# A Perceiver layer: the queries of tiles 5 to 15 projected in three rounded passes

## The reference

```python
x = x + xattn(layernorm(x), ctx_1024, lens, Wq, Wk, Wv, Wo, q_norm_w, k_norm_w)
x = x + attn(layernorm(x), w_qkv, w_out)      # sparse causal mask, 16 heads
x = x + ffn(layernorm(x), w_gate, w_up, w_down)   # 4-bit weights, 16-bit activations

def xattn(q, kv, lens, Wq, Wk, Wv, Wo, q_norm_w, k_norm_w):   # q (32,64,128), kv (32,1601,128)
    qh, kh, vh = heads(q @ Wq), heads(kv @ Wk), heads(kv @ Wv)   # 16 heads of 64
    qh, kh = rms_norm(qh, q_norm_w), rms_norm(kh, k_norm_w)
    scores = einsum('bhld,bhsd->bhls', qh, kh) / 8
    scores = where(arange(1601) < lens, scores, -1e9)
    return merge(softmax(scores) @ vh) @ Wo
```

## Time and profile before

| what | value |
|---|---|
| median of 3 executions | 2392.42 us (2389.41 to 2395.27) |
| the profiled execution, its own time | 2390.12 us |
| its span in the profile | 2388.3 us |
| array busy | 2322.5 us, 97% of the span, 16519 matmuls |
| VectorE, ScalarE, GpSimd busy | 2096.7, 1363.6, 1485.5 us |
| query stage: first to last carry in the array's timeline | 30.16 to 119.83 us |
| mean granted clock of the array | 0.997 |

### The profile page before, as it was taken

How to read it: one execution, slowest core, us unless ns; L and a number is a source line. 1 busy time by engine, 2 the same in 40 slices (tenths; PEclk the granted TensorE clock), 3 DMA queues, 4 the chain that set the end, 5 groups by cost and what they waited for, 6 DMA issues and landing times. The chain is left out here.

```text
span 2388.3 us, 57754 instructions
## 1 busy us (share of the span) xinstructions
PE 2322.5 (97%) x16519; PEld 1967.9 (82%) x16519; DVE 2096.7 (88%) x3382; ACT 1363.6 (57%) x2594; POOL 1485.5 (62%) x1069
## 2 busy tenths in 40 slices
PE   7989999999999999999999999999999998999988
PEld 4757888888888888888888888888888888878755
DVE  8799999999999999999999999999999998468777
ACT  5845555555555555555555555555555554355646
POOL 4556777777777777777777777777777773001100
PEclk9999999999999999999999999999999999999999
DMA  3522222222222222222222222222222214431000
GB/s 112 194 78 47 55 54 54 54 55 54 56 53 54 54 57 54 54 52 56 55 55 54 54 54 54 54 54 54 54 54 54 54 39 123 149 107 38 2 2 18
DMA packets 442654, 145.07 MB, mean 61 GB/s; under 512 B 365361, under 2 KB 425681, under 8 KB 442449
## 3 DMA queue, kind: packets, MB, share of 16 engines
q1 hardware_dynamic: 442432, 143.50, 24.2%
q10 hardware_dynamic: 144, 0.52, 0.1%
HBM read 109.17 MB, written 34.73 MB: 60 GB/s over the span
## 5 line engine op out<-in xcount | busy, mean ns | idle before, releaser
L472 POOL TENSOR_TENSOR probs<-arena,best_all 128x1024 f32 (+2 forms) x397 | 943.4, 2376 | 422.6 <-DVE best L849 402.8
L1114 PEld LDWEIGHTS u_ps<-rows,probs 128*128 128x128 f32 x6656 | 800.5, 192 | 55.8 <-issue 14.7
L1114 PE MATMUL u_ps<-rows,probs 128*128 (+1 forms) x6656 | 811.4, 275 | 10.1 <-ACT probs L677 5.0
L834 DVE SCALAR_TENSOR_TENSOR arena<-s_ps,mask,rrms 128x512 f32 (+2 forms) x832 | 603.4, 726 | 116.4 <-PE s_ps L978 115.0
L677 ACT ACTIVATE probs<-probs 128x1024 f32<-128x1024 f32 (+1 forms) x416 | 440.8, 1061 | 411.5 <-POOL probs L472 397.8
L809 DVE TENSOR_REDUCE ssq<-squares 128x16 f32<-128x1024 f32 (+2 forms) x416 | 490.2, 1178 | 34.2 <-ACT squares L635 33.2
L635 ACT ACTIVATE squares<-k_ps 128x512 f32<-128x512 f32 (+1 forms) x832 | 451.2, 591 | 40.9 <-PE k_ps L978 21.4
L849 DVE TENSOR_TENSOR best<-best,arena 128x1024 f32<-128x1024 f32 (+1 forms) x352 | 446.7, 1269 | 0.4 <-issue 0.2
L976 PE MATMUL k_ps<-w_hi,cT_hi 128*128 128x512 f32 (+1 forms) x832 | 362.4, 436 | 4.8 <-ACT squares L635 4.8
L629 ACT ACTIVATE cT_hi<-cT 128x128 fp32r<-128x128 f32 (+1 forms) x416 | 129.3, 311 | 370.3 <-DVE cT L800 370.2
L976 PE MATMUL s_ps<-q_hi,cT_hi 128*128 (+2 forms) x832 | 330.5, 397 | 3.2 <-DVE arena L834 3.0
(11 more groups left out here) (257 smaller groups left out, 2236.7 us busy)
## 6 DMA issues: line engine op xcount, KB each, us to landing
stage<-in_ctx SPq DMA_DIRECT2D x1536, 16.0 KB, 1.7
rows<-in_ctx SPq DMA_DIRECT2D x32, 768.0 KB
queries<-probs SPq DMA_DIRECT2D x16, 1024.0 KB, 4.1
q_plain<-queries SPq DMA_DIRECT2D x32, 512.0 KB, 3.3
best_all<-best_rows SPq DMA_DIRECT2D x31, 512.0 KB, 3.6
u_transposed<-uT_sb SPq DMA_DIRECT2D x124, 128.0 KB, 2.6
a_uT<-u_transposed SPq DMA_DIRECT2D x10, 1024.0 KB, 4.9
arena<-u_transposed SPq DMA_DIRECT2D x6, 1024.0 KB, 4.9
```

What stands on the lines that cost most here:

```text
L472: pool.tensor_tensor(probs[0:r, slot_of(c, PRING), :], scores_at(b, c), best_all[0:r, bass.ds((b % 2) * HL, HL)], ALU.subtract).then_inc(s ...
L834: dve.scalar_tensor_tensor(out=scores_at(p, c, h * HALF, HALF).rearrange("p (h l) -> p h l", l=L), in0=s_ps[h][0:r, :].rearrange("p (h l) ...
L1114: last = pe.matmul(u_ps[g // 3][:, at:at + UW], probs[0:r, s, g * P:(g + 1) * P], rows, start=(c == 0 and g % 3 == 0), stop=(c == NC - 1), ...
```

## The change

A constant `ROUNDED_FROM = 5` is added. Tiles 0 to 4 are projected as before. From tile 5 on each half is projected in three passes, like the keys: the high part of x by the high part of the weight, high by low, low by high. Where the operands come from:

- the high part of the weight is a ScalarE copy into the second half of `q_hi` in step 3, the low part a VectorE subtraction into the second half of `q_lo` in step 4;
- the high part of each tile of x is a ScalarE copy (128x128) into slot 11 or 12 of `cT_hi`, at the end of `query(i)` for tile i + 1, the low part a VectorE subtraction into `cT_lo`, at the end of its `query(i)`; the array waits for it ahead of the first half of tile i + 1.

The semaphores `w_hi_ready` and `w_ready`, so far used for the split of the key weight alone, count on for this.

```diff
--- before.py
+++ after.py
@@ -171,6 +171,7 @@
 KEYS_FROM = 5
 CHUNK = 4
 FREE_FROM = TILES - CARRY_Q
+ROUNDED_FROM = 5
 
 
 def each_step(eng, query, step, keys_from=KEYS_FROM):
@@ -330,6 +331,18 @@
         def part(late):
 
             return slice(EARLY * H, NC * H) if late else slice(0, EARLY * H)
+
+        def wq_of(part, h):
+
+            return part[:, HL + h * HALF:HL + (h + 1) * HALF]
+
+        def tile_x(t):
+
+            return xT[:, t % (2 * CHUNK) * P:(t % (2 * CHUNK) + 1) * P]
+
+        def tile_x_of(part, t):
+
+            return part[:, NC - 2 + t % 2, :]
 
         def carry_banks(t, k):
 
@@ -551,6 +564,17 @@
                 act.wait_ge(x_turned, j + 1)
                 act.activation(xT[:, (j % 2) * HALF:(j % 2 + 1) * HALF], x_ps[:, :], ACT.Copy).then_inc(xT_ready, 1)
 
+            def split_wq_hi():
+                act.wait_ge(wq_lens_in, 32)
+                act.activation(q_hi[:, HL:2 * HL], wq, ACT.Copy).then_inc(w_hi_ready, 1)
+
+            def split_x_hi(t):
+                act.wait_ge(xT_ready, t // CHUNK + 1)
+                act.wait_ge(w_ready, t - ROUNDED_FROM + 1)
+                if t - 2 >= ROUNDED_FROM:
+                    act.wait_ge(q_proj, 2 * (t - 2) + 2)
+                act.activation(tile_x_of(cT_hi, t), tile_x(t), ACT.Copy).then_inc(w_hi_ready, 1)
+
             def save_q(t):
                 act.wait_ge(q_proj, 2 * t + 1)
                 if t >= 8:
@@ -608,6 +632,10 @@
                     save_even(i - CARRY_Q, 1)
                 if i % CHUNK == 0 and i + 4 < TILES:
                     rough_layernorm(i // CHUNK + 1)
+                if i == ROUNDED_FROM - 2:
+                    split_wq_hi()
+                if ROUNDED_FROM <= i + 1 < TILES:
+                    split_x_hi(i + 1)
                 if i == 0:
                     act.activation(w_hi[:, :], u_sb[:, :], ACT.Copy).then_inc(w_hi_ready, 1)
 
@@ -756,6 +784,14 @@
                 at = (t % 8) * HL + HALF
                 dve.tensor_copy(q_ring[:, at:at + HALF], s_ps[1][:, :]).then_inc(q_saved[1], 1)
 
+            def split_wq_lo():
+                dve.wait_ge(w_hi_ready, 2)
+                dve.tensor_tensor(q_lo[:, HL:2 * HL], wq, q_hi[:, HL:2 * HL], ALU.subtract).then_inc(w_ready, 1)
+
+            def split_x_lo(t):
+                dve.wait_ge(w_hi_ready, 3 + t - ROUNDED_FROM)
+                dve.tensor_tensor(tile_x_of(cT_lo, t), tile_x(t), tile_x_of(cT_hi, t), ALU.subtract).then_inc(w_ready, 1)
+
             def save_odd(t, k):
                 dve.wait_ge(q_carried, 2 * t + k + 1)
                 if k == 0 and t >= 2:
@@ -790,6 +826,10 @@
                     layernorm_variance(i // CHUNK + 2, i % CHUNK)
                 if i % CHUNK == 1 and i + 3 < TILES:
                     layernorm_scale((i + 3) // CHUNK)
+                if i == ROUNDED_FROM - 1:
+                    split_wq_lo()
+                if ROUNDED_FROM <= i + 1 < TILES:
+                    split_x_lo(i + 1)
 
             def turn(p, n, c):
                 s = slot_of(c, RING)
@@ -992,8 +1032,15 @@
                 else:
                     pe.wait_ge(q_saved[h], t)
                     pe.wait_ge(q_squared, 2 * t - 1 + h)
-                at = t % (2 * CHUNK) * P
-                pe.matmul(s_ps[h][:, :], xT[:, at:at + P], wq[:, half(h)], start=True, stop=True).then_inc(q_proj, 1)
+                out = s_ps[h][:, :]
+                if t < ROUNDED_FROM:
+                    pe.matmul(out, tile_x(t), wq[:, half(h)], start=True, stop=True).then_inc(q_proj, 1)
+                else:
+                    if h == 0:
+                        pe.wait_ge(w_ready, 3 + t - ROUNDED_FROM)
+                    pe.matmul(out, tile_x_of(cT_hi, t), wq_of(q_hi, h), start=True, stop=False)
+                    pe.matmul(out, tile_x_of(cT_hi, t), wq_of(q_lo, h), start=False, stop=False)
+                    pe.matmul(out, tile_x_of(cT_lo, t), wq_of(q_hi, h), start=False, stop=True).then_inc(q_proj, 1)
 
             def turn_q(t):
                 pe.wait_ge(q_normal, t + 1)
```

## The result

| | before | after |
|---|---|---|
| median | 2391.73 us (7 executions, 2387.89 to 2395.27) | 2397.64 us (7 executions, 2396.06 to 2402.99) |
| ratio | | 1.0026 [1.0016, 1.0037] |
| profiled execution: own time, span | 2390.12, 2388.3 us | 2397.64, 2395.5 us |
| mean granted clock | 0.997 | 0.996 |

The kernel became slower by 0.26%, +6.2 us (3.8 to 8.8), where +2.0 was forecast. That the time came out as "no difference" is in part luck. Some 0.35 us of it lie outside the span in which the profile sees the program: time less span is 1.79 us in the profiled execution before and 2.14 after, and the other executions of each kernel repeat both within 0.1.

What follows compares the result with a forecast made beforehand. It took a loop through VectorE and ScalarE to bound the query stage's steps. Early costs +2.3, later steps -0.9 and ports +0.6 summed to +2.0 us on the 2392.42 us median: 2394.4 us, range 2387.0 to 2399.5.

Steps and rivals of the forecast that it cites:

- the loop: Query steps, tiles 8 to 15: VectorE and ScalarE need 6.43 us a step with the copy for x; -0.9 us.
- the array would like 6.56 - 0.5 = 6.06: Query steps from tile 8: without other engines, rounded passes would let the array do a step in 6.06 us.
- the array sets the pace: Rival, query stage: splits are covered, array keeps its 5.6 us less 0.95 for the weight's high part; 2387.7 us, chance 0.17.
- the waits for tiles 5 and 6: Steps 4 and 5: the array waits for VectorE's low parts, starting projections 1.29 and 1.17 us late.
- the shorter projections of tiles 5 to 7, some 0.4 us each: Early query steps: three rounded passes per half shorten these three projections, 1.2 us gained in all.
- Tiles 7 and 8 ... 0.1 us for the two tiles: Query stage: the low part of x releases the array at 2.89 us against 2.82, costing 0.1 us for both.
- the ports, +0.6: Steps 4 to 7: VectorE's low part of x contends with GpSimd's small rows in SBUF, 0.15 us for each of four tiles.
- The chance of 0.12 that this order turns: Rival, query stage: low part of x waits behind GpSimd's normalization, 1.4 us a tile; 2402.8 us with six tiles, chance 0.12.
- Behind it I find nothing that would absorb or enlarge a shift: After the query stage: any shift of its end moves batch 0's start and passes on unchanged.
- the prediction's own list: Signs of being wrong: steps of 6.1 us, over 1 us idle beyond tile 6, or scores' start and kernel's end moving differently.
- the last steps keep their length: Query stage's last steps, which have no projections: no change in length.
- the clock: Rival: two new idle stretches over 1 us in steps 4 and 5 bring a 6% dip over 20 us; 2395.6 us, chance 0.06.

Runs made afterwards that it cites:

- e2: Kernel before with tiles 5 to 15 projected in three rounded passes on key-weight parts, without splits or their wait (real projection left out); 2390.64 us, ratio 0.9999.
- f1: Kernel after with the parts of x made one or two steps earlier, in three slots, weight split unmoved; 2394.23 us, ratio 1.0010 to the kernel before.
- e3: Kernel before with three rounded passes on key-weight parts for tiles 5 to 15 (real projection left out), plus ScalarE's copy for x; 2391.97 us, ratio 1.0003.
- g4: Kernel after, unchanged, profiled a third time; low clock at 29 to 32 and about 38 to 44 us; own time 2399.8 us.
- g1: Kernel before, unchanged, profiled again; low clock (0.50) at 29 to 32 us; own time 2392.27 us.
- f5: Kernel after with the first two key-tile loads of batch 1 issued ahead of the last two query stores; 2398.76 us, ratio 1.0024 to the kernel before.
- g3: Kernel before, unchanged, profiled once more; full clock from 29 us to about 44 us; own time 2388.3 us.
- f3: Kernel after with x split earlier, rounding from tile 6, weight parts moved (low part on GpSimd), batch 1's first two loads earlier; 2390.59 us, ratio 0.9993 to before.

## Why the prediction was right and wrong

**Right in size, wrong in reason: the loop, -0.9 us.** Measured are -1.2 us from tile 8 (+3.35) to tile 15 (+3.09, with 0.95 taken out that a store's wait put in at tile 10). VectorE's sums of squares are 6.48, 6.49 and 6.28 us apart where 6.43 was worked out. But that the copy in ScalarE's chain makes this length is not what the runs show: without it there the steps are 6.29, 6.48 and 6.49 (e2, f1), and e3 loses 0.16 us to it in all, not 0.20 in each step. The agreement of 6.43 with 6.48 is luck: the slack of 0.33 us had been counted in VectorE's and ScalarE's rows alone, and GpSimd stands in the way as well. The other side of the comparison, "the array would like 6.56 - 0.5 = 6.06", was wrong too: it is 6.24, since its gain is 0.32 us a step, 0.24 in the two halves and 0.08 at the turn. For the same reason the rival "the array sets the pace" could not have brought 5.6 us; e2, the passes alone, wins 1.7 by the first pass.

**Right: the waits for tiles 5 and 6.** Forecast 0.95 + 1.29 = 2.24 at tile 5, measured 2.20; 1.17 for tile 6, measured 1.01 beyond tile 5 with 0.25 given back, 1.26 in all. The low part of x takes 0.30 us, the straight line's value. The high part of the weight, priced at 0.95, makes the first carry of tile 4's step start at 30.98 in place of 30.16 us, behind a wait of 1.06 for ScalarE's copies.

**Mis-sized: "the shorter projections of tiles 5 to 7, some 0.4 us each".** Between its first projection and its second carry the array needs 2.85 us (37.32 to 40.17) and needed 3.10 (35.12 to 38.22): 0.25 each, 0.45 less in all. The halves take 0.87 and 0.89 us there, above my 0.70 to 0.80. I had taken those from key passes that follow other passes; between two carries the first pass needs 0.31 to 0.34 us and the step from the last to the carry 0.33.

**Missed: "Tiles 7 and 8 ... 0.1 us for the two tiles".** I followed the low part of x to the array, and not what stands behind it on VectorE: the turn of a key tile, for which ScalarE's `cT_hi` waits, and behind that the copies that the carry needs. 0.5 us. What is queued behind a waiting instruction was named for ScalarE and not for VectorE.

**Mis-sized the other way: the ports, +0.6.** In the profile after all eleven low parts of x take 0.28 to 0.31 us. GpSimd's timeline in step 5, beside the low part's 43.80, shows the order: the low part starts while the last small row runs, and the normalization follows it.

```profile
43.42 0.54 POOL L498 TENSOR_TENSOR arena<-arena 128x16 f32<-128x16 f32 x1
44.03 1.90 POOL L504 TENSOR_TENSOR arena<-arena 128x1024 f32<-128x1024 f32 x1
```

The chance of 0.12 that this order turns was no fiction, though: in g4 it did, once.

**Failed: "Behind it I find nothing that would absorb or enlarge a shift".** The wait for the load of batch 1 enlarges the shift by 0.9, 0.9 and 1.4 us in the three profiles of the kernel after (waits of 1.21, 1.16 and 1.73 us against 0.27, 0.37 and 0.48 in those of before), and absorbs the whole gain of e2. By the prediction's own list this is a sign of being wrong: the start of the scores moved by 3.55 us and the end by 7.2. And "the last steps keep their length" misses 0.46 us in steps 17 to 19, where VectorE's copy waits for a store.

Summed for the profile after, in us: 3.35 at tile 8, -1.2 for the loop, +0.95 for ScalarE's wait at tile 10, +0.46, +0.9, and -0.3 in batch 0: +4.2. The wait at tile 10 is met in an execution of the kernel before as well:

```profile
66.24 0.60 ACT L613 ACTIVATE probs<-u_ps 128x512 f32<-128x512 f32 x1 [0.84 <-DMA queries<-probs]
```
```profile
64.41 0.60 ACT L589 ACTIVATE probs<-u_ps 128x512 f32<-128x512 f32 x1 [1.03 <-DMA queries<-probs]
```

The second row is of g1, the kernel before. But it is not to be taken off the change's account. At full clock neither profile of the kernel before has it and both of the kernel after do (0.84 and 1.34 us). All ten profiles that reach tile 9 by 0.8 us or more late have it, and of the four others only e2 (0.42). So a shift of the stage brings it, by this association, whether the change or the clock made the shift. The change costs +4.2 us by batch 1 in an execution at full clock, where +2.0 was forecast.

**What goes beyond that is, as far as it can be told, the clock,** priced as a rival at 0.06. Its condition, two new idle stretches of over 1 us, was named rightly. What was wrong is that I gave it as a case of its own, worth an average of 6% over 20 us, when it comes on top of the forecast in some executions. Where the first low stretch is met, the kernel before loses 1.3 us by tile 5 and 0.9 at tile 10, 2.2. The kernel after, whose 4.2 have the wait at tile 10 in them, loses 0.6 (g4, 37.94) to 0.8 by tile 5 (f5, 38.16), then 1.5 for the second, and in g4 1.8 for the ports and 1.5 for the third. That is 0.1 us more than the kernel before for f5 and 3.2 for g4. If half of the executions are hit, 0 to 1.6 us are added to the mean difference: with 4.2 some 4 to 6 us, and 0.35 outside the span, where 3.8 to 8.8 was measured. This is an estimate from two hit profiles. The three profiles of each kernel lie apart by 5.0 us at batch 1 and by 6.3 in their own times, in the mean. That the waits bring the second low stretch is an association in seven profiles (three of three with them, none of four without), no proof. The size of the loss is thus accounted for within its interval, but how much of it the clock makes stays open, for which three executions of each are too few.

f1 fits this reading: it takes away the wait for tile 6 and shortens that for tile 5, and the ratio falls from 1.0026 to 1.0010. It also moves the copy for x; the two were not tested apart.

## What to carry to other kernels

An engine that is busy all the time may be filled by a loop that runs through the others: trace one step from its last release back to itself, and count the idle fractions in the loop, before matmul time is called gain. A length that fits is no proof of the loop, though: take the instruction out of it and look at more than one step. Here 6.48 us came back without the copy. A small instruction put at the end of an engine's step is priced by what stands behind it and by who waits for that; in gaps of the steps ahead the same instructions started the scores 2.5 us earlier (122.36 against 124.88 us), and by the medians cost some 3.8 us less, within intervals that overlap. And a single profile places a shift only to about 2 us here: look at the granted clock stretch by stretch, and at a second execution of the kernel before, before a difference is called the change's.

## What the runs showed of the hardware

- The same instructions from 28 to 32 us met a granted clock of 1.00 in some executions and 0.50 in others, worth 1.3 us. Just before it the array had stood still for 2.54 us in profiles of either kind (28.12 before, 28.02 in g1), so the idle time alone does not decide it. And a low stretch costs by its place: 1.3 us at 28 to 32 us, 1.0 to 1.3 between 2019 and 2064 us, nothing from 23.4 us (g3).
- Three passes of 128x512 in fp32r follow each other by 0.31 and 0.23 us (37.32, 37.63, 37.86), and with the change to the carry a half takes 0.87, where the fp32 half took 0.96 to 1.05. Rounding saves 0.1 to 0.2 us a half, less than the passes' own rate suggests.
- A VectorE subtraction of 128x128 took 0.30 us when ahead of GpSimd's long multiplication and 1.98 when 0.39 us behind its start (g4); behind GpSimd's 128x1024 subtraction it took 0.78 (f3). Both times it ended 0.14 us after GpSimd's instruction.
- A VectorE operation with one input of 128x16 took 0.17 us alone and 0.22 to 0.45 in the steps in which GpSimd's 128x256 subtraction was running, and ended 0.03 us after it each time; behind the 128x1024 multiplication it took 0.70 in the kernel after (45.26, GpSimd's ending at 45.93).
